# Attention, LayerNorm and linear kernel on 8 cores: a weight load moved behind the small-weight stage, and projection jobs run whole instead of in halves

## What is computed

```python
qkv = x @ W_attn + b_attn                       # [2048, 3072]
q, k, v = split(qkv)                            # 16 heads of 64
att = softmax(causal(q @ k.T / 8))
y = (att @ v) @ W_proj + b_proj
x = layernorm(x + y)
W_real = unfold(G1_R, G2_R); W_imag = unfold(G1_I, G2_I)     # 512 x 512 each, from small factors
x_real, x_imag = split(x)
f = concat(x_real @ W_real.T - x_imag @ W_imag.T + bias_real,
           x_real @ W_imag.T + x_imag @ W_real.T + bias_imag)
out = layernorm(x + f)
```

## Time and profile before

| | |
|---|---|
| runs | 1395.65 us median of 3 (1394.23 to 1455.9) |
| the profiled execution | 1393.38 us |
| its span, slowest core (core 5) | 1391.8 us; the eight cores 1383.6 to 1391.8 |
| PE busy | 1136.9 us, 82% |
| ACT busy | 711.9 us, 51% |
| DVE busy | 508.9 us, 37% |
| mean granted clock of PE, core 5 | 0.902 |
| 960 matmuls of projection jobs into ps_g (L467) | 264.7 us busy, 31.4 us idle before them |
| 640 exponentials (L567) | 593.6 us busy |

### The profile page before, as it was taken

One profiled execution on the slowest core, in us unless ns is written; L12 is line 12 of the kernel. 1 busy time (PEld: TensorE's weight loads), 2 busy tenths in 40 slices (PEclk: granted clock), 3 DMA queues, 4 the chain that ended last, 5 costly groups with the idle time before them and its releaser, 6 DMA issues.

```text
span 1391.8 us, 23510 instructions; the slowest of 8 cores (1383.6 to 1391.8 us)
## 1 busy us (share of the span) xinstructions
PE 1136.9 (82%) x8930; PEld 543.6 (39%) x8930; DVE 508.9 (37%) x1015; ACT 711.9 (51%) x842; POOL 117.4 (8%) x137
## 2 busy tenths in 40 slices
PE   2089987887887888898988998788878878789896
PEld 1055433433433434443335543333334333444332
DVE  1145323223223222364664532322322232146475
ACT  1100276766876878465110027677677677835411
POOL 3010010000000000032231000000000000003232
PEclk9999998898998995998997999899898898699999
DMA  6966410000000006330235200000000000532022
GB/s 193 277 117 101 11 39 17 16 1 16 16 1 24 24 1 99 122 122 1 106 127 164 88 1 1 16 16 1 16 17 1 16 17 1 92 133 110 1 121 121
DMA packets 99957, 82.41 MB, mean 59 GB/s; under 512 B 84864, under 2 KB 85000, under 8 KB 98824
## 3 DMA queue, kind: packets, MB, share of 16 engines
q1 hardware_dynamic: 88024, 36.75, 11.6%
q0 software_dynamic: 10912, 37.76, 9.1%
q10 hardware_dynamic: 912, 6.39, 1.5%
HBM read 52.59 MB, written 24.12 MB: 55 GB/s over the span
## 4 chain that ended last, share of the span: by engine, by line
PE 51%; ACT 18%; DVE 11%; issue 11%; DMA 7%; DVEq 0%; ACTq 0%; POOL 0%; SPq 0%; POOLq 0%
ACT p L567 15%; PE ps_g L467 14%; PE ps_big L547 9%; PE ps_big L401 8%; PE ps_y L620 8%; PE ps_big L798 7%; DMA wstage<-w_attn 4%; DVE x_tok L814 3%; DMA x_tok<-x_in 3%; DVE stats_sb L821 2%; PE ps_y L364 2%; DVE qp L483 2%; DVE stats_sb L825 1%; DMA xstage<-x_in 1%; PE ps_big L785 1%
## 5 line engine op out<-in xcount | busy, mean ns | idle before, releaser
L567 ACT ACTIVATE p<-ps_big,consts 128x1024 bf16<-128x1024 f32 (+3 forms) x640 | 593.6, 985 | 395.2 <-PE ps_big L547 388.3
L547 PE MATMUL ps_big<-qp,kp 64*128 64x512 bf16 (+3 forms) x1280 | 242.0, 395 | 93.8 <-ACT p L567 88.7
L467 PE MATMUL ps_g<-x_feat,W_sb 128*128 128x512 bf16 x960 | 264.7, 404 | 31.4 <-DVE kp L483 19.1
L584 DVE TENSOR_TENSOR pd<-p,mask_sb 128x256 bf16<-128x256 bf16 x256 | 74.4, 291 | 366.9 <-ACT p L567 279.9
L620 PE MATMUL ps_y<-v_all,p 128*128 128x65 bf16 x3840 | 196.3, 204 | 6.3 <-ACT p L567 6.2
L620 PEld LDWEIGHTS ps_y<-v_all,p 128*128 128x128 bf16 x3840 | 151.7, 103 | 85.7 <-issue 77.2
L547 PEld LDWEIGHTS ps_big<-qp,kp 64*128 64x128 bf16 x1280 | 66.2, 95 | 279.3 <-issue 270.2
L467 PEld LDWEIGHTS ps_g<-x_feat,W_sb 128*128 128x128 bf16 x960 | 83.0, 102 | 105.1 <-issue 51.0
L835 ACT ACTIVATE mv_sb<-mv_sb,consts 128x1 f32<-128x1 f32 x64 | 18.9, 295 | 203.7 <-DVE mv_sb L829 203.7
L798 PE MATMUL ps_big<-Wbig_sb,x_feat 128*128 128x512 bf16 x512 | 120.6, 390 | 0.0
L798 PE MATMUL ps_big<-Wp_sb,x_feat 128*128 128x512 bf16 x512 | 117.7, 384 | 1.1 <-DVE x_feat L741 1.1
(11 more groups left out here) (67 smaller groups left out, 666.5 us busy)
## 6 DMA issues: line engine op xcount, KB each, us to landing
xstage<-x_in POOLq DMA_DIRECT2D x32, 512.0 KB, 5.3
x_tok<-x_in POOLq DMA_DIRECT2D x8, 2048.0 KB, 8.9
out<-x_tok SPq DMA_DIRECT2D x32, 512.0 KB, 2.7
wstage<-w_attn ACTq DMA_DIRECT2D x4, 1536.0 KB, 17.0
wstage<-w_attn SPq DMA_DIRECT2D x4, 1536.0 KB, 20.2
ystage_d<-yst SPq DMA_DIRECT2D x12, 512.0 KB, 3.8
Wp_sb<-w_proj POOLq DMA_DIRECT2D x8, 256.0 KB, 26.4
Wbig_sb<-w2r_d POOLq DMA_DIRECT2D x8, 128.0 KB, 2.4
```

Of the source, the lines that this page charges most:

```text
L467: return t.matmul(bank[:], W_sb[:, cc * 3072 + j0:cc * 3072 + j0 + 128], x_feat[:, cc * T + tg * 512:cc * T + (tg + 1) * 512], start=(cc = ...
L547: return t.matmul(ps_big[:, off:off + ln], kpb[e * 64:(e + 1) * 64, kk * 128:(kk + 1) * 128], qpb[e * 64:(e + 1) * 64, pos:pos + ln], star ...
L567: return a.activation(o, i, AF.Exp, bias=consts[:, 0:1], scale=0.125)
L584: return v.tensor_tensor(po_, pp, mm_, ALU.mult)
```

## The change

Two edits. The `w_attn` section is moved, in the text and so on every queue, behind the small-weight stage, and all four transfers of a wave are issued on ACT's queue. The halves of a projection job are joined: a list of 8 whole jobs takes the place of 16 halves, and since `emit_pv` still runs one entry per slot, slots 0 to 7 get a whole job each and slots 8 to 15 none.

```diff
-    prev = ([], 0, 0)
-    for wave in range(2):
-        ...
-            S.emit("ac" if i < 2 else "sy", lambda a, cc=cc, i=i: a.dma_start(
-                out=wstage[:, i * 3072:(i + 1) * 3072],
-                in_=w_attn[cc * 128:(cc + 1) * 128, :]),
-                waits=w_extra, inc="q_wa", amt=16)
-        ...
     for fi, wdst in enumerate([w2r_d, w2i_d]):
         ...
     v_w2done = S.val("q_w2")
     v_w3done = S.val("q_w3")
 
+    prev = ([], 0, 0)
+    for wave in range(2):
+        w_extra = []
+        if wave == 1:
+            w_extra = [("ac", S.val("ac")), ("dv", S.val("dv"))]
+        for i in range(4):
+            cc = wave * 4 + i
+            S.emit("ac", lambda a, cc=cc, i=i: a.dma_start(
+                out=wstage[:, i * 3072:(i + 1) * 3072],
+                in_=w_attn[cc * 128:(cc + 1) * 128, :]),
+                waits=w_extra, inc="q_wa", amt=16)
+        v_wa_ld = S.val("q_wa")
+        for i in range(4):
+            ...                      # casts by ACT (i even) and DVE (i odd), as before
+    v_wa_ac = S.val("ac")
+    v_wa_dv = S.val("dv")
 ...
-                    def half(lo, which=which, j0=j0, dstbuf=dstbuf, bcol=bcol,
-                             tg=tg, par=par, bname=bname, bank=bank):
+                    def job(which=which, j0=j0, dstbuf=dstbuf, bcol=bcol,
+                            tg=tg, par=par, bname=bname, bank=bank):
                         vpe = 0
-                        for cc in range(lo, lo + CC // 2):
+                        for cc in range(CC):
 ...
-                        if lo > 0:
-                            def evq(v, ...):
-                            ...
-                            return (tg if which == 1 else None, vdv)
-                        return None
-                    jobs.append(lambda half=half: half(0))
-                    jobs.append(lambda half=half: half(CC // 2))
+                        def evq(v, ...):
+                            ...
+                        vdv = S.emit("dv", evq,
+                                     waits=[("pe", vpe), ("ac", v_bqk),
+                                            G["qk%d" % par]], inc="dv")
+                        G[bname] = ("dv", vdv)
+                        return (tg if which == 1 else None, vdv)
+                    jobs.append(job)
```

More of the change, by code:

```diff
@@ L254, in build @@
     v_w3done = S.val("q_w3")
+    prev = ([], 0, 0)
[11 more added lines that the diff above has]
+        for i in range(4):
+            cc = wave * 4 + i
+            if i % 2 == 0:
+                S.emit("ac", lambda a, cc=cc, i=i: a.copy(
+                    W_sb[:, cc * 3072:(cc + 1) * 3072],
+                    wstage[:, i * 3072:(i + 1) * 3072]),
+                    waits=[("q_wa", v_wa_ld)], inc="ac")
+            else:
+                S.emit("dv", lambda v, cc=cc, i=i: v.tensor_copy(
+                    W_sb[:, cc * 3072:(cc + 1) * 3072],
+                    wstage[:, i * 3072:(i + 1) * 3072]),
+                    waits=[("q_wa", v_wa_ld)], inc="dv")
+    v_wa_ac = S.val("ac")
+    v_wa_dv = S.val("dv")
     S.emit("po", lambda g: g.dma_start(
@@ L479, in half, with evq @@
                                 vpe = r
-                        if lo > 0:
[L481 to L489, removed]
-                            return (tg if which == 1 else None, vdv)
-                        return None
-                    jobs.append(lambda half=half: half(0))
-                    jobs.append(lambda half=half: half(CC // 2))
+                        def evq(v, dstbuf=dstbuf, tg=tg, bcol=bcol,
+                                bank=bank):
+                            return v.tensor_scalar(
+                                dstbuf[:, tg * 512:(tg + 1) * 512], bank[:],
+                                bqk[:, bcol:bcol + 1], None, ALU.add)
+                        vdv = S.emit("dv", evq,
[4 more added lines that the diff above has]
+                    jobs.append(job)
             return jobs
```

## The result

The changed kernel takes 1493.0 us (median of 9 runs, 1489.0 to 1512.0), against 1394.4 us for the kernel before (10 runs on the same chips): a ratio of 1.071, 95% interval 1.0694 to 1.0727. The forecast was 1467 with a range of 1430 to 1500 and 0.88 for slower: right in sign and range, with a loss of 99 us where 73 were forecast. Single executions of either kernel run some per cent longer at a lower granted clock, and the ratios leave these out. The profiled execution took 1494.3 us, its slowest core (core 5 again) 1492.8 us, 101 more than before.

The account below looks back on a forecast made before the run. PE was taken to bound slots 0 to 7, with PE and ACT level in 8 to 15. Per pair 6.5 - 1.6 = 4.9 us, +69 over 14 pairs, +3 setup, on 1393.4: 1465, forecast as median 1467, range 1430 to 1500.

Parts of the forecast that it names:

- The bound of each kind of slot: Attention pairs: PE sets the pace in slots 0 to 7; PE and ACT are level in 8 to 15, ACT alone without jobs.
- Slots 8 to 15: Attention pairs: without half jobs the mean falls from 19.05 to about 17.4 us, 1.6 us less per pair.
- Pair 7: The pair without jobs before the change: slots 8 to 15 took 17.53 us at granted clock 0.58, the model for 17.4.
- The bound of 2.00 us per slot: Slots 8 to 15: at granted clock 1.00 a slot without a job repeats after 2.00 us, 3.0 us off per pair.
- Slots 0 to 7: Attention pairs: whole jobs of 1.73 us and seven copy gaps of 1.00 us add 6.5 us per pair.
- The worse rival: Attention: PE's low clock in every pair adds 46 us on top, giving 1513 us; chance 0.15.
- The not-slower rival: Slots 0 to 7: PE's 3.7 us idle per pair takes the jobs in, 1395 to 1400 us; chance 0.10.
- the main case: Whole kernel: net 3.2 to 6.4 us more per pair, 1436 to 1492 us; chance 0.72.
- the bound of 8: Slots 0 to 7: the range for added time per pair goes up to 8 us, above the 6.5 taken.
- The setup: Moved load before attention: second wave lands at 67 us, x transposes start +3 us later, with -2 and +9 as bounds.
- one queue's share: Setup, second wave of w_attn: on one queue its DMA share would fall from 0.70 toward 0.5 while POOL's loads last.
- placement theory: Attention: a half job is nearly free under the exponentials of slots 8 to 15, costs its full length in slots 0 to 7.

## Why the prediction was right, and where its terms were off

**The bound of each kind of slot.** Right in the main. PE set the pace in slots 0 to 7 and ACT in slots 8 to 15, and moving the jobs took from the second less than it gave to the first. ACT is not the whole bound of slots 8 to 15, though: without jobs they take 1.6 us less at granted clock 1.00 than at 0.61 (15.98 and 17.57 in the run with the jobs alone).

**Slots 8 to 15**, 1.6 us less per pair: right to the tenth (266.7 to 244.4 us over 14 pairs). Pair 7 was a good model, because it had the low clock as well: 0.61 and 0.70 now, against its 0.58. The bound of 2.00 us per slot, 3.0 off, would have needed the full clock.

**Slots 0 to 7**, 6.5 us more: 8.3 was measured, a little outside the 8 to which the range was let go. The mechanism, job plus gap, was right (the run with the half copy shows the gap), and two terms were short. The first is a mix of two ways of measuring. The gap of 1.00 us was read between a row's end and the next row's start, and rows of the timeline include the matmul's modelled end; the job of 1.73 was read from the chain, which does not. On the timeline a whole job is 1.89. Seven gaps at 0.16 each are 1.1 us per pair. The second is the clock. I let the first half of the first job run at the low clock and the second at full; the row shows 3.52 us for both, where I had 1.68 + 0.86 = 2.54: 1.0 us per pair. So pair 1 took 27.77 us and not 25.7, and it had been 0.3 us shorter than the mean before the change, which leaves the 1.8 missed. Pair 8, whose granted clock was 1.00, took 25.61; that this is next to my 25.7 for a pair that starts slow is chance. At 14 pairs the miss is 25 us; less the 2.4 that slots 16 to 23 lost, where I had forecast no change, it is the 22 us between the 69 forecast for attention and the 91 measured. Where the 8.3 lie: PE is busy for 7.7 us more per pair and idle for only 0.6 more. PE's idle time before all the jobs of the kernel rose from 31.4 to 40.3 us, not "well above": most of a gap is filled with scores and V products, which have to be done in any case.

**The worse rival, the clock all through,** came in part, and not in the time added. Slots 16 to 23 stayed at 12.7 us per pair, and the low clock at a pair's start went no further than the first job. The mean granted clock of core 5 fell from 0.902 to 0.854, in slots 8 to 15: there it was 0.91 or 1.00 and is 0.61 or 0.70. By my own signs ("wrong if the pairs' low-clock stretches change by much") that speaks against the prediction, but its 17.4 us for slots 8 to 15, taken from pair 7, already had this clock in it. It costs: at 1.00 a pair would take up to 1.6 us less, 22 us in all (an estimate, 14 times the difference of the two rows of the run with the jobs alone).

**The not-slower rival** asked for the 3.7 us of idle time to take the jobs in. PE's idle time in slots 0 to 7 rose instead, to (387.5 - 327.7) / 14 = 4.3 us per pair.

**The range.** 1493.0 lies in 1430 to 1500, but 1 us above the main case, which ended at 1492. The net per pair was 91.2 / 14 = 6.5 us, and the main case had 3.2 to 6.4. Those two ends do not follow from the rule that stands beside them: 6.5 and 1.6 moved by half of the way to their bounds give 2.6 at the low end and 6.2 at the high end with the bound of 8, or 7.9 with that of 11.5. That the range held is in part luck: the time lies in the room that was left for the worse rival.

**The setup**, +3 us: 7.0 measured, inside the bounds of -2 and +9. The step that failed was the first one, that the product would still start at 15.94: the small factors came 10 us late behind ACT's transfers. The second wave was then issued at 48.5 and not 38.5, and landed at 71.4 and not 67. Its 21.6 us against 27.8 before go with an engine share of 93.0% for its queue from 50 to 71 us: POOL's loads were done by then, so my worry over one queue's share had nothing to act on here. In the run with only the queue changed it had. The Trainium skill ("DMA: Bandwidth & Descriptors", Queues, rings and completion order) says that queues with work take turns on each DMA engine, and that run agrees in direction: the wave had 60.1% on one queue where it had 69.8% on two, short of the 50% that I feared, and took 3.5 us longer. By the same page of the Trainium skill (Issuing engines are not separate DMA queues) issuing on several engines saves nothing but issue time; the time of the kernel, at ratio 1.0001, fits this, while the wave's share and the small loads that landed 8 us later do not. From the landing to the first transpose it was 12.0 us, where I had 10.5.

**What the experiments added.** My placement theory of a price per half job was too simple. Whole jobs in every second slot cost 57 us, whole jobs in each of slots 8 to 15 cost 2. As I read it, one slot's scores are all that is in hand, so with a job in every slot ACT's exponentials run beside PE's job each time (a pitch of 2.90 us), while with jobs in every second slot PE must first wait for ACT in the slot without one, and ACT then waits for PE in the slot with one (5.40 us for two slots, row by row above). And a job needs a copy's length of other work behind it, or PE waits for the bank. Whether more room for scores, or a second bank for the jobs, would lift these limits was not tried.

## What to carry to other kernels

Filler work on an in-order engine should be spread evenly over the steps in which the other engine has the most to do. In this kernel its place and its evenness counted for more than the size of its pieces: whole jobs cost 2 us with one in each of slots 8 to 15, 57 in every second slot and 91 in slots 0 to 7. Where one PSUM bank serves it, count the copy's time after every piece that ends a group and ask what runs beside it. Before moving a block of code, list what each queue then has to wait for, and what that in turn waits for: here 6 MB waited for a few kilobytes, by the order on DVE and by the queue that made the kilobytes late. Lengths from two views should not be added up without a look at whether both include the end of the pipeline. And a stretch in which ACT is the bound can still be longer at a low clock of PE.

## What the hardware showed that I had not expected

With four 1.5 MB transfers on ACT's queue, the product that needs four small loads (40 KB together, issued at 1.1 to 2.2 us on SP's queue) started at 24.4 and 25.8 us; with two of the four on SP's queue behind the small loads, it started at 15.9, and at 8.3 in the run with the other setup, where the mask and the identity stand ahead of ACT's two. Two score matmuls that use 64 rows each, for the two heads of a pair, run side by side: four of 128x512 took 0.61 us on the timeline at the full clock, where four job matmuls of the same width, with 128 rows, took 1.02.
